# Two-layer cross-attention kernel on one core: a new order in the opening, in the odd items of the second attention, around item 44, and context's low parts on GpSimd

## What is computed

```python
ln_out = layernorm(x, ln1_s, ln1_b)                       # layer 0, self attention: phase A
q, k, v = split(ln_out @ w_qkv + b_qkv)
x = x + attention(q, k, v, ltor_mask) @ w_ao + b_ao       # 16 heads of 32
q = layernorm(x, ln2_s, ln2_b) @ w_q + b_q                # layer 0, cross attention: phase B
k, v = split(encoder_states @ w_kv + b_kv)
x = x + attention(q, k, v, cross_mask) @ w_co + b_co
x = x + gelu(layernorm(x, ln3_s, ln3_b) @ w1 + b1) @ w2 + b2     # MLP
a = _layer_norm(audio_kv, ln_gamma, ln_beta)              # layer 1, gated attention: phase D
scores = (x @ Wq.T) (a @ Wk.T)^T * scale                  # per head
out = softmax(scores) (a @ Wv.T) @ Wo.T
x = x + tanh(gate) * out
```

```python
scores = einsum('bhqd,bhkd->bhqk', q, k) / sqrt(HD)
scores = scores * mask - 10000.0 * (1.0 - mask)
probs = softmax(scores)
```

## Time and profile before

| | |
|---|---|
| median of 3 runs | 1086.4 us (1083.62 to 1086.55) |
| profiled execution, its own time | 1087.28 us |
| its span | 1085.7 us |
| TensorE's granted clock | 1.00 over the whole span |
| busy: TensorE, its weight load | 1066.5 us, 924.1 us |
| busy: VectorE, ScalarE, GpSimd | 820.6 us, 704.0 us, 483.4 us |
| DMA, share of the 16 engines | 54.9% |

### The profile page before, as it was taken

How to read it: one execution, slowest core, us unless ns; L and a number is a source line. 1 busy time by engine, 2 the same in 40 slices (tenths; PEclk the granted TensorE clock), 3 DMA queues, 4 the chain that set the end, 5 groups by cost and what they waited for, 6 DMA issues and landing times.

```text
span 1085.7 us, 24226 instructions
## 1 busy us (share of the span) xinstructions
PE 1066.5 (98%) x8741; PEld 924.1 (85%) x8741; DVE 820.6 (76%) x1303; ACT 704.0 (65%) x2355; POOL 483.4 (45%) x361
## 2 busy tenths in 40 slices
PE   8999999999999999999999999999999999999998
PEld 7889888888888888887898888888888998888886
DVE  8788777777888787888867667767697467777667
ACT  5787778677778787786444444444455276666676
POOL 4776555566777776767513122113032233333210
PEclk9999999999999999999999999999999999999999
DMA  7366666577777777564252151341647647777621
GB/s 248 104 190 209 202 206 192 187 190 223 221 217 216 222 216 227 180 193 139 85 155 98 59 174 59 117 141 53 214 136 257 229 127 207 223 209 210 195 61 60
DMA packets 145927, 185.92 MB, mean 171 GB/s; under 512 B 17952, under 2 KB 88848, under 8 KB 145808
## 3 DMA queue, kind: packets, MB, share of 16 engines
q1 hardware_dynamic: 145808, 184.37, 54.9%
HBM read 122.59 MB, written 61.73 MB: 170 GB/s over the span
## 4 chain that ended last, share of the span: by engine, by line
PE 66%; DVE 11%; DMA 7%; ACT 6%; POOL 4%; SPq 4%; issue 3%; DVEq 0%; ACTq 0%; POOLq 0%
PE psum L895 17%; PE psum L1094 15%; PE psum L1075 14%; PE psum L887 7%; PE psum L1014 6%; POOL prob L2267 3%; PE psum L913 2%; ACT prob L1409 2%; PE psum L991 2%; DMA ln_tile<-stream 2%; DMA normalised<-ln_tile 2%; DVE ln_tile L1739 2%; PE psum L933 2%; DVE negmax L1817 1%; SPq L558 1%
## 5 line engine op out<-in xcount | busy, mean ns | idle before, releaser
L895 PE MATMUL psum<-inputs_hi,weights_hi 128*128 128x256 f32 x768 | 224.2, 292 | 2.0 <-POOL inputs_lo L2253 1.4
L895 PE MATMUL psum<-inputs_lo,weights_hi 128*128 128x256 f32 x768 | 217.1, 283 | 0.0
L895 PE MATMUL psum<-inputs_hi,weights_lo 128*128 128x256 f32 x768 | 216.9, 282 | 0.0
L2267 POOL TENSOR_TENSOR prob<-prob,mask_bias 128x1024 f32<-128x1024 f32 x64 | 153.1, 2413 | 93.8 <-DVE prob L1804 93.2
L895 PEld LDWEIGHTS psum<-inputs_hi,weights_hi 128*128 128x128 f32 x768 | 146.6, 191 | 8.5 <-issue 2.9
L1817 DVE TENSOR_REDUCE negmax<-prob 128x8 f32<-128x1024 f32 x96 | 115.8, 1212 | 49.3 <-POOL prob L2267 49.1
L1409 ACT ACTIVATE prob<-prob,negmax 128x128 f32<-128x128 f32 x384 | 148.3, 391 | 0.5 <-DVE negmax L1817 0.5
L895 PEld LDWEIGHTS psum<-inputs_lo,weights_hi 128*128 128x128 f32 x768 | 147.0, 191 | 0.2
L895 PEld LDWEIGHTS psum<-inputs_hi,weights_lo 128*128 128x128 f32 x768 | 146.9, 191 | 0.0
L2253 POOL TENSOR_TENSOR inputs_lo<-inputs_transposed,inputs_hi 128x512 fp32r<-128x512 f32 x70 | 93.5, 1357 | 94.3 <-DVE inputs_hi L1777 60.5
L1409 ACT ACTIVATE prob_blocks<-prob,negmax 128x128 f32<-128x128 f32 x304 | 117.8, 391 | 19.4 <-DVE negmax L1817 19.3
(11 more groups left out here) (138 smaller groups left out, 2657.0 us busy)
## 6 DMA issues: line engine op xcount, KB each, us to landing
weights_whole<-weights_in SPq DMA_DIRECT2D x80, 256.0 KB, 3.8
prob_turned<-prob_blocks SPq DMA_DIRECT2D x38, 512.0 KB, 3.0
prob<-prob_turned SPq DMA_DIRECT2D x152, 128.0 KB, 3.5
inputs_transposed<-normalised SPq DMA_DIRECT2D x120, 128.0 KB, 2.8
normalised<-ln_tile SPq DMA_DIRECT2D x24, 512.0 KB, 2.8
context<-row_sums_spread SPq DMA_DIRECT2D x188, 64.0 KB, 2.1
stream<-residual SPq DMA_DIRECT2D x42, 256.0 KB, 2.9
ln_tile<-stream SPq DMA_DIRECT2D x32, 256.0 KB, 4.1
```

The lines of the kernel that those rows point to most:

```text
L895: mm = pe.matmul(ps[:, bank, GT * part:GT * part + GT], w[:, slot, c, o], a[:, buf, c, :], start=c == 0 and i == 0, stop=c == KC - 1 and i ...
L2267: pool.tensor_tensor(half, half, mb.unsqueeze(1).to_broadcast([128, 8, T]), ALU.add).then_inc(s_biased, 1)
```

## The change

It moves instructions between places and engines; what is computed and how often stays the same.

1. `LO_BY_POOL` takes in items 1 to 27: their `context_lo`, two instructions of 128x256, goes from VectorE to the start of GpSimd's step.
2. In phase B's odd items VectorE does `inverse_sums(g-1)` ahead of `context(g-2)`; in its even items (up to 26) `turn_blocks(g)` stands ahead of the layer norm `statistics`.
3. Items 30 and 31 are written anew. On VectorE the mask comes ahead of the reciprocal and of `context_lo`; in item 31 `row_max` stands apart from its second half, and gelu 0 is split around a copy. On ScalarE `exps(30, 0)` comes ahead of `hidden_out(1)` and `exps(31, 0)` ahead of `hidden_out(3)`, `tanh(0)` moves back. On TensorE `w2(0)` comes ahead of `row_sums(31)`.
4. Weight unit 14 is split ahead of 13. GpSimd does not split 14 before gelu's third low part is there (`s_glo` 3), and splits 13 after it; unit 15 and the low and high parts of the MLP's second fill come one chunk later. `w2` waits for each weight chunk by itself.
5. Opening: GpSimd waits for the normalised second group before it splits unit 1's last chunks; it has no weight split in item 1 and three in item 2; `prob_out(0, 3)` on VectorE comes ahead of `row_max(1, 1)`.
6. Item 44: ScalarE copies the row sums ahead of `context_hi`, and makes the fill's high part ahead of the first exponentials.

```diff
-CHUNKS += [(u, c) for u in (12, 13, 14, 15, 16, 17, 18, 19) for c in range(KC)]
+CHUNKS += [(u, c) for u in (12, 14, 13, 15, 16, 17, 18, 19) for c in range(KC)]
-LO_BY_POOL = tuple(range(32, 44))
+LO_BY_POOL = tuple(range(1, 28)) + tuple(range(32, 44))
...
 pe w2
-                if group.first == 0 and j % 2 == 0:
-                    pe.wait_ge(s_wlo, max(LO_COUNT[W2_UNIT[n], c] for c in range(KC)))
+                if group.first == 0:
+                    pe.wait_ge(s_wlo, LO_COUNT[W2_UNIT[n], (j * chunks + chunks - 1) % 4])
...
 pe last_steps_of_b
                 w1(4)
+                w2(0)
                 row_sums(31)
                 transpose_prob(31, 0)
                 transpose_prob(31, 1)
-                w2(0)
...
 act step
+                if g == 44:
+                    row_sums_out(g - 1)
-                if st.prev and not late:
+                if st.prev and not late and g != 44:
                     row_sums_out(g - 1)
-                early = g == 0 or (st.fill in TURNED and g not in (1, 28, 29))
+                early = g == 0 or (st.fill in TURNED and g not in (1, 28, 29, 44))
...
 act last_steps_of_b, as it is after
+                context_hi(28, 0)
+                context_hi(28, 1)
+                row_sums_out(29)
+                hidden_out(0)
+                prob_out(29, 0)
+                split((12, 0))
+                split((12, 1))
+                exps(30, 0)
+                hidden_out(1)
+                prob_out(29, 2)
+                exps(30, 1)
+                exps(30, 2)
+                context_hi(29, 0)
+                context_hi(29, 1)
+                exps(30, 3)
+                row_sums_out(30)
+                hidden_out(2)
+                prob_out(30, 0)
+                tanh(0)
+                split((12, 2))
+                split((12, 3))
+                exps(31, 0)
+                hidden_out(3)
+                prob_out(30, 2)
+                exps(31, 1)
+                exps(31, 2)
+                exps(31, 3)
...
 act, MLP's first chunks
-                if (g, jp) == (0, 5):
+                if (g, jp) == (0, 6):
                     for c in range(KC):
                         split((15, c))
-                    fill_scale(mlp_fill(1))
...
 dve step
+                ahead = phase == B and b % 2 == 1
+                if ahead:
+                    inverse_sums(g - 1)
...
+                    prob_out(0, 3)
...
+                blocks_first = phase == B and b % 2 == 0 and g not in BY_PE
+                if blocks_first:
+                    turn_blocks(g)
                 if later_ln:
                     statistics(st.later)
-                if g not in BY_PE:
+                if g not in BY_PE and not blocks_first:
                     turn_blocks(g)
...
 dve last_steps_of_b, as it is after
+                context(28, 0)
+                context(28, 1)
+                make_mask_bias(30)
+                mask_scores(30, 0)
+                inverse_sums(29)
+                mask_scores(30, 1)
+                context_lo(28, 0)
+                context_lo(28, 1)
+                prob_out(29, 1)
+                row_max(30, 0)
+                row_max(30, 1)
+                prob_out(29, 3)
+                normalise(mlp_fill(1))
+                tanh_argument(0)
+                stream(28)
+                context(29, 0)
+                context(29, 1)
+                make_mask_bias(31)
+                mask_scores(31, 0)
+                mask_scores(31, 1)
+                inverse_sums(30)
+                context_lo(29, 0)
+                context_lo(29, 1)
+                row_max(31, 0)
+                prob_out(30, 1)
+                row_max(31, 1)
+                gelu_hi(0)
+                prob_out(30, 3)
+                gelu_lo(0)
+                tanh_argument(1)
+                stream(29)
...
 pool
-                if g:
-                    for chunk in (STEPS[A][0].weights if g == 1 else []) + st.weights:
+                if g > 1:
+                    for chunk in (STEPS[A][0].weights + STEPS[A][1].weights if g == 2 else []) + st.weights:
                         split(chunk)
...
+                attention_residual(31)
+                pool.wait_ge(s_glo, 3)
                 for c in range(KC):
-                    split((13, c))
-                attention_residual(31)
+                    split((14, c))
...
+            pool.wait_ge(s_xhat, 4)
...
-                if (g, jp) == (0, 5):
-                    for c in range(KC):
-                        split((15, c))
+                if (g, jp) == (0, 6):
                     fill_lo(mlp_fill(1))
+                    split((15, 0))
+                    split((15, 1))
...
                     inverse_deviation(FILLS_OF_MLP[1][0])
+                    split((15, 2))
+                    split((15, 3))
```

More of the change, by code:

```diff
@@ L1562, in last_steps_of_b @@
             def last_steps_of_b():
-                for b in (14, 15):
-                    g = 16 + b
-                    if b == 14:
-                        context_hi(g - 2, 0)
-                        context_hi(g - 2, 1)
-                    else:
-                        tanh(0)
-                    row_sums_out(g - 1)
-                    hidden_out(2 * b - 28)
-                    prob_out(g - 1, 0)
-                    for c in range(2 * b - 28, 2 * b - 26):
-                        split((12, c))
-                    hidden_out(2 * b - 27)
-                    prob_out(g - 1, 2)
-                    exps(g, 0)
-                    exps(g, 1)
-                    exps(g, 2)
-                    if b == 14:
-                        context_hi(29, 0)
-                        context_hi(29, 1)
-                    exps(g, 3)
+                context_hi(28, 0)
[25 more added lines that the diff above has]
+                exps(31, 3)
                 context_hi(30, 0)
@@ L1678, in act_program @@
             for c in range(KC):
-                split((14, c))
+                split((13, c))
             for p in range(5, NG * NPAIR):
@@ L1942, in step @@
                     mask_scores(g, 0)
-                if st.ends and not late and g - 1 not in WHOLE and g != 44:
+                if st.ends and not late and not ahead and g - 1 not in WHOLE and g != 44:
                     inverse_sums(g - 1)
@@ L1992, in step @@
                     turn_inputs(STEPS[A][1].fill)
-                if st.prev and g - 1 in BY_PE and g not in (28, 33):
+                if st.prev and g - 1 in BY_PE and g not in (1, 28, 33):
                     prob_out(g - 1, 3)
@@ L2170, in dve_program @@
                     gelu_lo(p - 1)
+                    if g == 0:
+                        fill_hi(mlp_fill(1))
                     tanh_argument(p)
@@ L2193, in dve_program @@
                     turn_inputs(mlp_fill(1))
-                    fill_hi(mlp_fill(1))
                 if jp == (4 if g == 1 else 5) and 0 < g < NG - 1:
```

26 lines of the change are left out of this document (2 added, 24 removed).

## The result

The changed kernel took 1096.2 us (median; 1093.4 to 1100.2) against 1086.7 for the kernel before (1083.6 to 1088.2): a ratio of 1.0094, 95% interval 1.0077 to 1.0111. It is slower by nearly 1%, and the prediction, 1084.5 with a range to 1089.8, was wrong. The profiled execution of the changed kernel took 1099.1 us, its span is 1097.7.

The account below looks back on a forecast made before the run. TensorE was taken as the bound, busy 1066.5 of 1085.7 us. Terms -1.6 - 0.6 + 1.7 - 1.4 = -1.9 us took the profiled 1087.28 to 1085.4, by the median's ratio 1084.5; range 1078.5 to 1089.8.

Parts of the forecast that it names:

- MLP chunks (step 4): MLP: finer waits of `w2` and the other order of units 13 and 14 cost 0 if GpSimd is in time.
- Items 30 and 31: End of phase B: `project_out(28)` 4.0 us late through low parts under the bias and exponentials; net +1.7 us, bounds -4.7 and +6.6.
- Rival N: Items 30 and 31: no queue, VectorE gets between GpSimd's instructions; part -2.4, sum -6.0, 1080.4 us; chance 0.32.
- The later waits: MLP, gelu 1 and 2: without GpSimd's splits beside them, stalls of 1.03 and 0.94 us plus refills go, -2.2 us.
- rival S: MLP: shared interface decides everywhere, two stalls stay, 2.3 us of new ones come; part +6.6, sum +3.0, 1089.4 us; chance 0.12.
- The granted clock is 1.00 throughout, so no clock effect is in play: Whole kernel: TensorE's clock stays at its full level, so no clock term enters the sum.
- The 0.15 us that the prediction adds to each stall for a refill: TensorE's stalls: each also costs a pipeline refill, estimated at 0.15 us on top.
- Phase B: Odd items: earlier reciprocal removes TensorE's waits, two thirds of 2.5 us gained, -1.6; bounds -2.9 and +1.0; period near 30 us.
- rival Z: Phase B: GpSimd's period holds, its bias starts when it did, the moves give 0; sum -0.3, 1086.1 us; chance 0.09.
- Phase A and opening: Opening's 0.46 us wait goes, `context_lo` in phase A is covered by GpSimd's idle time; sum -0.6, bounds -2.0 and +0.6.
- Item 44: End of phase D: earlier row-sum copy and high part on ScalarE remove two TensorE waits; -1.4 us, bounds -1.5 and -0.3.

Follow-up runs that it names:

- the item 44 experiment: The kernel before with ScalarE's new order of item 44 alone; 1087.1 us, ratio 0.9995.
- its siblings: The experiments' kernels that have the same phase A as the changed kernel, each with some other edit taken back or moved; no single measured time.
- the base: The changed kernel with all of the end of phase B as before (ScalarE's and VectorE's orders, `w2(0)`, units 13 and 14); 1082.4 us, ratio 0.9964.

## Why the prediction was wrong

**The step that failed: "MLP chunks (step 4)".** It put the new order of units 13 and 14 at nothing "so long as GpSimd is done in time". It followed the splits of one engine and never asked when the raw weights arrive, nor what stands behind a split that waits. ScalarE splits too, its splits of item 31 stand ahead of `prob_out(31, 2)` and the high part of context 31, and the unit that they now take is loaded last. The trace of before held all of it: the loads of unit 14 go out at 503.11 there, behind the row sums, and ScalarE's splits of unit 13 ran from 501.57 (SyncE's queue and ScalarE, kernel before):

```profile
503.11 2.53 SPq L617 DMA_DIRECT2D weights_whole<-weights_in  x4
...
501.57 2.18 ACT L1337 ACTIVATE weights_hi<-weights_whole 128x512 fp32r<-128x512 f32 x4
```

So even with nothing else moved the splits had to wait; and the change also moved 2.9 us of `w2(0)` ahead of the row sums on which the loads' turn in the queue hangs. Measured with early loads: 7.4 us in the medians. GpSimd, which the step did follow, took 12.2 us for its eight splits, from 523.8 on, where the prediction has 11.4 from near 515, and TensorE waited under 0.1 us for them directly. Counted from the start of item 30, the changed kernel is 4.5 us late at `project_out(30)`, where the prediction has 4.0, and 13.0 late at `project_out(31)`: the 8.5 us between them are in no term of its sum. The Trainium skill, Perfetto Trace Analysis, section "Per-instruction lifecycle: what the profiler-reported window actually captures", says that semaphore waits, and on DMAs the whole data movement, fall outside the window that a slice shows. This trace agrees: the four issues show as 1.80 us at 511.07, and it is ScalarE's idle time of 5.67 us that tells when the first had landed.

**Items 30 and 31: the place and the size were right, the cause only in part.** The prediction has `project_out(28)` 4.0 us late for `hidden_out(1)` behind four exponentials; it came 3.2 later relative to item 30, at a wait of 2.81. But it derived this from VectorE's low parts growing under the bias, and single edits show that ScalarE's order alone makes a wait of 2.19 us, and VectorE's order alone none; with both it is 2.81, so the low parts' share is some 0.6 us. The low parts did grow, to 4.08 and 4.03 us for two in the changed kernel. The Trainium skill, SBUF — State Buffer, section "SBUF: two separate sides", has an exclusive lock on the second port pair, held for a whole instruction; the growth agrees with it. What it costs is another matter: on the path little or nothing. Rival N, which had these items at -2.4 because the low parts find a gap, was wrong in its mechanism; VectorE's half of the change gains, though for another reason: gelu 0 starts earlier and no longer holds the reciprocal up. The waits of 0.85 and 1.21 us of `row_sums(30)` and `row_sums(31)` go, and waits of 0.27 and 1.14 us for a copy of VectorE come.

**The later waits.** The prediction let the waits of `w2(2)` and `w2(5)` go, -2.2, since GpSimd's splits no longer lie beside gelu 1 and 2. Both waits went, gelu 2's first two pieces taking 0.69 and 0.43 us beside no split, but two others came (`w2(4)` and `w2(7)`, 0.80 and 1.39 us in the changed kernel): rival S's mechanism, at the price of the term's gain and no more. It wasn't what decided.

**"The granted clock is 1.00 throughout, so no clock effect is in play"** was read from the kernel before and carried over to one with longer waits. In the changed kernel part of the work ran at the lower level, behind the waits of 1.17 and 1.08 us in item 31 and behind that of 6.91. The kernel before isn't free of it either: its profiled execution shows 1.00, but 8 of the 27 measured beside the item 44 experiment show 0.997 or 0.998. The 0.15 us that the prediction adds to each stall for a refill, without a row, measures about 0.1: `w2(2)` of before takes 3.04 us behind its wait, `w2(3)` 2.91 without one.

**Phase B** was forecast at -1.6, bounds -2.9 and +1.0. Between items 16 and 30 it gained 2.7 us in the changed kernel's trace and 3.2 to 4.6 in its siblings. GpSimd's idle time ahead of the bias went as forecast, from 33.7 us in items 16 to 29 to none. But the period did not hold (rival Z): from one odd item's bias to the next it fell from 30.0 to 29.4 us (items 19 to 27). The term was mis-sized. TensorE's idle time in these items was 3.3 us before and 0.8 in the kernel with VectorE's order alone, which gained 4.0; so some 1.5 us of the gain don't stand in the rows as idle time, and what they were stays open.

**Phase A and opening** was forecast at -0.6, bounds -2.0 and +0.6. At item 4 the changed kernel stands at +0.7, its siblings with the three splits at +0.4 to +0.9: -0.3 from the opening, +1.0 from item 1 to item 4, at or past the upper bound. The prediction had seen the cause (three splits push item 3's bias back "by about as much as item 2 gains") but charged it against the 0.9 that item 2 gained, and not once more in item 3, where `v_out` waits behind the bias.

**Item 44** was forecast at -1.4; the traces give -1.24 to -1.25, and both waits of the earlier trace rows are gone.

Put together, in the two profiled executions: -0.3 at item 1, +1.0 by item 4, +1.4 in the rest of phase A (taken for chance), -2.7 in phase B, +13.9 from item 30 to phase D, -1.2 at item 44: +12.1. These two executions differ by 11.8 us, the medians by 9.5; the 2.3 between are the scatter of single executions. What stays open is how what the four edits at the end of B do to each other (4.4 us in the traces, 9.5 in the medians) divides between the loads, the low parts and the clock. VectorE's order alone gained 2.7 us in the medians and 1.1 in the trace behind item 30; its profiled execution was already 1.3 us ahead of the base's at item 30, where the two kernels are still the same.

## What to carry to other kernels

When an order of units changes on the engines that consume them, write down for each when its load is issued and on what that place in the queue hangs, before asking whether an engine has time for it. For every instruction that can now wait, list what stands behind it on its own engine: here it was the split of a weight that the seventh chunk of the MLP is the first to need, ahead of a copy that TensorE needed at once. And an instruction that takes five times as long (4.07 us for two low parts in place of 0.84) costs nothing until somebody waits for it, so follow the chain to TensorE before pricing it, and again when a second edit shortens that chain.

## What the hardware showed that I had not expected

TensorE's granted clock fell to 0.50 (1.2 GHz) behind waits at the end of phase B and stayed there while TensorE was already working again: from about 494.3 to 497.7 us and from 514.8 to 521.6 in the changed kernel. The cost is seen in the same instructions at either level: the 32 matmuls of `times_v(31)` 1.93 us against 1.08, and the 12 of `w2(2)` in the kernel with the old unit order 4.29 against the 2.91 of its `w2(0)`. It doesn't follow each wait alike. Behind the same 2.81 us at `project_out(28)` the clock fell in the kernels with early loads, with the old unit order and with `prob_out` first, and not in the changed kernel, which had it fall behind the waits of 1.17 and 1.08 us in item 31. Behind 2.19 us (ScalarE's order alone) it fell, behind the 1.42 that follow in the same kernel it did not. Behind the 2.29 us of the two kernels named below it fell as well. So such a wait may cost more than it shows, up to 1.7 us for a stretch of 3.4 us in which TensorE works throughout (an estimate, half of the stretch), or nothing more.

The waits of these kernels also move by chance. Kernels that are the same up to item 30 reach it, in their profiled executions, between -0.6 and -4.5 us against the kernel before. In two kernels, the one with the units changed over alone and that of item 44, a VectorE instruction took 1.78 us in place of 0.69 where GpSimd's addition of a residual, which waits for a DMA, began 0.3 us ahead of it, and the reciprocal behind it came 1.1 us late. In the kernel before the same addition begins 0.4 us behind that instruction, which takes 0.69.
